# Line products of the first two tiles moved from the last slot into the second half of the slot before it, in pairs

## The chip, the cores and the metric

The kernel runs on one core of one Trainium2 chip. The core has five engines that run at the same time and wait for each other by semaphores: TensorE (matrix products; PE in the profile, its weight loads PEld), VectorE (DVE), ScalarE (ACT), GpSimd (POOL) and SyncE (SP), which here starts the DMAs. The metric is the device time of one launch in microseconds (us); lower is better.

## What is computed

The input x is [4, 1024, 128]. A local-attention feed-forward block of two layers is added to it at half weight, then a global attention layer with a memory, then the feed-forward block again. The change is in the global attention layer. Cut to what matters there:

```python
qkv = (x @ qkv_w.T + qkv_b).reshape(B, T, 3, H, dh)     # B 4, T 1024, H 16, dh 8
attn = softmax(causal(einsum('bhtd,bhsd->bhts', q, k) * scale))
seq_out = einsum('bhts,bhsd->bhtd', attn, v)
w1, w2 = x_prev @ w1w.T, x @ w2w.T                      # [B, T, H, 4]
write_lines = exterior(w1, w2)                          # 6 numbers, divided by their norm
r1, r2 = x @ r1w.T, x @ r2w.T
read_lines = exterior(r1, r2)
outer = Jw[..., :, None] * Jw[..., None, :]             # Jw from write_lines, 6 x 6 a head
M_all = decayed cumulative sum of outer over positions  # before each position
score_M = sum(einsum('bhti,bhtij->bhtj', rd, M_all) * rd)
gated = mean(sigmoid(mem_score * mem_scale) * gate)
return (seq_out + gated * mem_val) @ out_w.T + out_b
```

So the layer has two halves: an ordinary causal softmax attention, and a memory of outer products of "lines", each line being a normalised exterior product of two 4-vectors.

## The kernel before, in words

The layer is `global_attention_pass`. After the projections come two passes over the attention scores, woven together in TensorE's order. The work is cut in 16 slots (`SLOTS`): slot n is batch n // 4 and four heads. Pass 1 (`fill`, line 1712 and on) computes scores so that VectorE can take each query's maximum; pass 2 computes scores again, with the maxima folded in, for ScalarE's exponentials and the value products. A slot of pass 2 has 12 units (`U2`), each a block of 128 keys and 512, 384, 256 or 128 queries. In this text (n, u) is unit u of slot n. Widths by u: 512, 384, 256, 128, 512, 512, 512, 512, 128, 256, 384, 512.

For a unit (n, u), TensorE's order is: the scores of the next unit in two halves of two banks each (`scores`, lines 1745, 1750, 1754), each half waiting until ScalarE has read the same half of the unit before; then the value products of (n, u) (`values`, line 1769), which wait for both of ScalarE's exponentials of that unit. Between these stand pass 1's products (`produce`), which run 23 uses ahead, so that they end in unit 5 of slot 14. ScalarE does `exp` (line 2289) twice a unit, copies the finished sums (`copy_out`, line 2296) after units 0 and 4, and does the inverse roots named below.

The memory half works by tiles of 128 positions; for tile k, `w` 0 is the written line and 1 the read one. The steps are:
- `line_items` (lines 1784 and 1786, TensorE): an item is one batch of one (k, w): two f32 products of 192 columns. Tile 0 has items 0 to 7 and tile 1 items 8 to 15. Item n waits until VectorE has multiplied item n - 2. Item 0 waits for all of pass 1.
- VectorE copies one half of an item (line 2064) and multiplies it by the other (2004). After four items GpSimd's `subtract` (2231) makes the lines, VectorE squares them (2075) and sums (2010), ScalarE's `inverse(k, w)` takes the inverse root (2342, 2345), VectorE's `clip` bounds it (2014) and GpSimd's `normalise` multiplies (2243).
- GpSimd's `outer_products(k)` (2254) makes the outer products in the memory of v_all. For k = 1 it waits for all value products.
- TensorE's `tails` (1799), VectorE's `advance` (2058) and SP's `pass_state` (2491) carry the state from one tile to the next.

Every engine works its own list in order. The first two tiles' steps are written out by hand, woven into slot 15; from tile 2 on each engine runs `body(t)`, behind the slots, and TensorE's memory products (1810) and lines of tile t + 2 stand in it. The items of tiles 0 and 1 run in slot 15, one after each half of the scores, in units 0 to 7; `tails(0)` runs after unit 9, and the four inverses on ScalarE after the exponentials of units 4, 5, 9 and 10. GpSimd's list begins with a memset of the state (2259), which waits for the scores of slot 14, then `subtract(0, 0)`, `subtract(0, 1)`, `normalise(0, 0)`, `normalise(0, 1)`, `outer_products(0)`, `subtract(1, 0)`, `subtract(1, 1)`, and so on. VectorE's list is items 0 to 5, squares and sum (0, 0), items 6 and 7, squares and sum (0, 1), items 8 and 9, `clip(0, 0)`, items 10 and 11, `clip(0, 1)`, items 12 and 13, squares and sum (1, 0), items 14 and 15, squares and sum (1, 1), `advance(0)`, `clip(1, 0)`, `clip(1, 1)`.

The small arrays of these steps lie in the ring of three query/key buffers (`kq`), in parts that slots 13 and 14 have finished with.

Of the kernel before, what the change touches and what calls it, by code (L numbers as in the profile page):

```python
# [15 lines left out]
B, T = 4, 1024  # L16
# [1410 lines left out]
SLOTS = B * GROUPS  # L1427
# [5 lines left out]
S_TILES = T // TILE  # L1433
# [85 lines left out]
LINE = 6  # L1519
LROWS = AH * LINE  # L1520
ITEMS = 2 * B
# [2 lines left out]
PAIRS_6 = LINE * LINE  # L1524
HB = AH * B
HALF_READ = 9
TAILS_AT = 9
BEHIND = 3
INVERSES_AT = (4, 5, 9, 10)
CHUNK_ORDER = tuple(range(0, CHUNKS, 2)) + tuple(range(1, CHUNKS, 2))  # L1530
EARLY = CHUNKS // 2

# [17 lines left out]
def global_attention_pass(nc, C, K, A, later_keys, y, v_all, kq, probs, scratch, o_all, den_all, x):  # L1550
# [11 lines left out]
    U2 = P2_STEPS  # L1562
    QK_DMAS, M_DMAS, O_DMAS = 4 * len(JOINED), 2 * PARTS, GROUP + 1
    with ExitStack() as ctx:
# [17 lines left out]
        squares = sb("ln_s", [P, 2, CHUNK])  # L1582
# [9 lines left out]
        shared = Arena(kq[:, :, :, :].rearrange("p k w t -> p (k w t)"))  # L1592
# [1 line left out]
        shared.at = 2 * T + TILE * 2  # L1594
        left = shared.take(4 * 2 * N).rearrange("p (n c) -> p n c", n=4)
        line = shared.take(2 * HB * LINE).rearrange("p (w h b c) -> p w h b c", w=2, h=AH, b=B)
        square = shared.take(2 * HB * LINE).rearrange("p (w x c) -> p w x c", w=2, x=HB)
        ssq = shared.take(2 * HB).rearrange("p (w x) -> p w x", w=2)
        inv = shared.take(2 * HB).rearrange("p (w x) -> p w x", w=2)
        state = shared.take(2 * GROUPS * STATE_ROWS).rearrange("p (k q n) -> p k q n", k=2, q=GROUPS)  # L1600
        first = Arena(early[:, :])
# [38 lines left out]
        def item(k, w, b):  # L1640
            return ITEMS * k + B * w + b
# [32 lines left out]
        def _(pe):  # L1674
# [100 lines left out]
            def line_items(k, w, b):  # L1775
                n = item(k, w, b)
                c = b * PAD + 1 + k * TILE
                out = ps[:, LINES + n % 2, 0:4 * N].rearrange("p (f c) -> p f c", c=N)
                if n == 0:
                    pe.wait_ge(C["p1_free"], C.after("p1_free", USES))  # L1780
                if n == 2 * ITEMS:
                    wait(pe, "ml_state", 1)
                wait(pe, "ml_mul", n - 1)
                nc.tensor.matmul(out[:, 0:4:3, :], y[:, c - 1 + w:c - 1 + w + TILE], A["wlines"][:, 4 * w:4 * w + 2, :], start=True,
                                 stop=True, skip_group_check=True)
                nc.tensor.matmul(out[:, 1:3, :], y[:, c:c + TILE], A["wlines"][:, 4 * w + 2:4 * w + 4, :], start=True, stop=True,
                                 skip_group_check=True).then_inc(C["ml_proj"], 1)
# [103 lines left out]
                if 0 <= i < 2:  # L1891
                    inverse_spread(i)

            def items(n, first):
                if n == SLOTS - 1 and first < 2 * ITEMS:
                    line_items(first // ITEMS, first % ITEMS // B, first % B)

            for m in range(2):
                centre(m)
# [18 lines left out]
            for n in range(SLOTS):  # L1918
                for u in range(U2):
                    ahead = (n, u + 1) if u + 1 < U2 else (n + 1, 0)  # L1920
                    if ahead[0] < SLOTS:
                        scores(*ahead, 0)
                    for use in uses_after(n, u, 0):
                        produce(use)
                    items(n, 2 * u)
                    if ahead[0] < SLOTS:
                        scores(*ahead, 1)
                    for use in uses_after(n, u, 1):
                        produce(use)
                    items(n, 2 * u + 1)  # L1930
                    values(n, u)
                    for use in uses_after(n, u, 2):
                        produce(use)
                    if n == SLOTS - 1 and u == TAILS_AT:
                        tails(0)
# [19 lines left out]
        def _(dve):  # L1955
# [204 lines left out]
            for use in range(USES):  # L2160
                n, f = use_of(use)
# [3 lines left out]
                take_max(n, f)  # L2165
                if f == FILLS - 1:
                    neg_max(n)
            dve.wait_ge(C["p2_scores"], C.after("p2_scores", 2 * U2 * (SLOTS - 1)))
            first_items(0, 6)
            first_squares(0, 0)  # L2170
            first_items(6, 8)
# [29 lines left out]
        def _(gp):  # L2201
# [53 lines left out]
                                        w.unsqueeze(3).to_broadcast([P, HB, LINE, LINE]),  # L2255
                                        w.unsqueeze(2).to_broadcast([P, HB, LINE, LINE]), ALU.mult).then_inc(C["ml_outer"], 1)

            gp.wait_ge(C["p2_scores"], C.after("p2_scores", 2 * U2 * (SLOTS - 1)))
            nc.gpsimd.memset(state[:, :, :, :], 0.0).then_inc(C["ml_set"], 1)

            def body(t):
                if valid(t + 1):
# [4 lines left out]
                    normalise(t + 2, 0)  # L2267
                    normalise(t + 2, 1)

            for t in range(-2, S_TILES + 2):  # L2270
                body(t)
            wait(gp, "ml_m", USES_M * LAST)
            for i in range(CHUNKS):
# [6 lines left out]
        def _(act):  # L2280
# [58 lines left out]
            def inverse(k, w):  # L2339
                wait(act, "ml_ssq", 2 * k + w + 1)  # L2340
                wait(act, "ml_unit", 2 * k + w - 1)
                nc.scalar.activation(inv[:, w, :], ssq[:, w, :], ACT.Ln, bias=K["norm_bias"][:, 0:1], scale=NORM_SCALE
                                     ).then_inc(C["ml_log"], 1)
                wait(act, "ml_log", 2 * k + w + 1)
                nc.scalar.activation(inv[:, w, :], inv[:, w, :], ACT.Exp, bias=K["norm_shift"][:, 0:1], scale=-0.5
                                     ).then_inc(C["ml_inv"], 1)
# [68 lines left out]
            for n in range(SLOTS):  # L2415
                for u in range(U2):
                    exp(n, u)
                    if u == 0 and n >= 1:
                        copy_out(n - 1, 1)
                    if u == 4:  # L2420
                        copy_out(n, 0)
                    if n == SLOTS - 1 and u in INVERSES_AT:
                        inverse(*divmod(INVERSES_AT.index(u), 2))
            copy_out(SLOTS - 1, 1)
            for t in range(S_TILES - 2):
                body(t)
# [92 lines left out]
    n = CHUNKS  # L2519
# [344 lines left out]
```

## Time and profile before

| what | us |
|---|---|
| median of 3 runs | 1938.73 (1938.09 to 1938.75) |
| the profiled execution | 1937.65 |
| its span in the profile | 1935.8 |
| TensorE busy | 1876.7 (97%) |
| VectorE busy | 1609.8 (83%) |
| ScalarE busy | 1500.5 (78%) |
| GpSimd busy | 918.2 (47%) |

The profile is one execution. Its times are microseconds from the start of the span; L12 is line 12 of the kernel. The timeline gives for each engine when an instruction (or a run of like ones, xN) starts and how long it takes; starts of two instructions that follow each other without idling tell what the first one occupies, which is less than its duration, since ends overlap the next start. In square brackets stands how long the engine idled before and who ended it. The two score passes take from about 715 to 1149 us; slot 14 begins near 1092 and slot 15 near 1115.

### The profile page before, as it was taken

What the parts mean: (1) busy time and instruction counts of PE and PEld (TensorE: products, weight loads), DVE (VectorE), ACT (ScalarE), POOL (GpSimd) and SP (SyncE); (2) the same over time, 40 slices, a digit from 0 to 9 for tenths busy, and PEclk for the clock granted to TensorE, in tenths of its full rate; (3) what the DMA queues carried; (4) which work ended last, traced back from release to release, by engine and by line L of the source; (5) the groups of instructions that cost most, each with busy time, mean ns of one, the idle gap of its engine ahead of it and who ended that gap; (6) DMA issues with size and microseconds to landing.
All of it is one profiled execution on the core that took longest, in us unless ns stands there. A gap on an engine that the chain in (4) does not pass through costs nothing. (4 is left out here: it accounts for less than half of the span.)

```text
span 1935.8 us, 61266 instructions
## 1 busy us (share of the span) xinstructions
PE 1876.7 (97%) x22612; PEld 1114.6 (58%) x22612; DVE 1609.8 (83%) x5464; ACT 1500.5 (78%) x4122; POOL 918.2 (47%) x550
## 2 busy tenths in 40 slices
PE   7999999999999989999999999899999999999999
PEld 3777763577775343444444358536777635777754
DVE  6899975899995679999999859869999658999945
ACT  5999994799997353777777754459999947999973
POOL 2788860588882040000000036428888505888820
PEclk9999999999999996999999999999999999999999
DMA  6212220122121040111111000002122201221311
GB/s 186 49 44 50 46 67 6 31 48 50 45 65 26 6 154 29 42 41 42 42 42 41 25 6 2 2 10 53 45 49 49 64 6 32 47 50 44 68 23 44
DMA packets 76154, 85.63 MB, mean 44 GB/s; under 512 B 17151, under 2 KB 50515, under 8 KB 75731
## 3 DMA queue, kind: packets, MB, share of 16 engines
q1 hardware_dynamic: 75663, 81.70, 16.8%
q8 instruction: 182, 2.98, 0.6%
q14 instruction: 113, 0.93, 0.2%
q10 hardware_dynamic: 196, 0.02, 0.0%
HBM read 21.16 MB, written 8.39 MB: 15 GB/s over the span
## 5 line engine op out<-in xcount | busy, mean ns | idle before, releaser
L336 ACT ACTIVATE probs<-probs,negmax 128x128 f32<-128x128 f32 x1024 | 402.0, 402 | 1.1 <-DVE negmax L411 0.6
L2289 ACT ACTIVATE gprobs<-ps_global 128x1024 f32<-128x1024 f32 (+3 forms) x384 | 291.4, 811 | 125.0 <-PE ps_global L1754 102.4
L291 POOL TENSOR_TENSOR rot<-rot 128x1024 f32<-128x1024 f32 x128 | 302.5, 2363 | 143.2 <-DVE rot L381 143.2
L297 POOL TENSOR_TENSOR qk<-rot,cnorm 128x1024 f32<-128x1024 f32 x128 | 243.8, 1905 | 172.8 <-issue 149.0
L304 POOL TENSOR_TENSOR probs<-probs,iden 128x1024 f32<-128x1024 f32 x128 | 242.8, 1897 | 45.7 <-DVE iden L419 45.0
L1984 DVE TENSOR_REDUCE maxes<-ps_global 128x1 f32<-128x512 f32 (+2 forms) x384 | 222.0, 638 | 10.3 <-PE ps_global L1717 6.5
L411 DVE CUSTOM_DVE_ANT_0 probs<-ps_attn,masks 128x128 f32<-128x128 f32 x1024 | 226.2, 285 | 0.7 <-issue 0.5
L336 ACT ACTIVATION_READ_ACCUMULATOR probs<-probs,negmax 128x1 f32 x1024 | 204.7, 200 | 0.0
L1712 PE MATMUL ps_global<-kq 48*128 48x512 bf16 (+3 forms) x768 | 196.9, 345 | 7.2 <-DVE maxes L1984 1.8
L2219 POOL CAST m_parts<-m_turn 32x128 bf16<-32x128 f32 x16 | 4.5, 280 | 363.3 <-DVE m_turn L1998 363.3
L377 DVE TENSOR_TENSOR rot<-ps_attn,rotary 128x512 f32<-128x512 f32 x256 | 174.9, 683 | 2.1 <-PE ps_attn L202 1.6
L1769 PE MATMUL ps_global<-gprobs,v_all 128*9 128x512 f32 (+3 forms) x1536 | 160.5, 490 | 1.7 <-ACT gprobs L2289 1.7
L271 PEld LDWEIGHTS ps_attn<-probsT,v_first 128*64 128x64 f32 x2048 | 103.7, 137 | 97.7 <-ACT probsT L357 93.9
L255 PEld LDWEIGHTS ps_attn<-ident,probs 128*128 128x128 f32 x1024 | 120.3, 141 | 67.0 <-issue 64.4
L638 ACT ACTIVATE ln<-ps_attn,vecs_sb 128x512 f32<-128x512 f32 (+2 forms) x96 | 65.6, 683 | 115.9 <-PE ps_attn L600 71.7
L387 DVE TENSOR_REDUCE ssq<-sq 128x16 f32<-128x1024 f32 x128 | 154.8, 1209 | 0.3
L1980 DVE CUSTOM_DVE_ANT_0 ps_global<-ps_global,later 128x384 f32<-128x384 f32 (+1 forms) x256 | 152.2, 652 | 2.7 <-PE ps_global L1712 1.7
L1712 PEld LDWEIGHTS ps_global<-kq 48*128 48x128 bf16 x768 | 58.8, 94 | 160.2 <-DVE maxes L1984 86.4
L1745 PE MATMUL ps_global<-kq 51*128 51x512 bf16 (+3 forms) x768 | 145.3, 329 | 2.7 <-ACT gprobs L2289 1.9
L224 PE MATMUL ps_attn<-ident,qk 128*128 128x128 f32 x1024 | 141.0, 281 | 6.0 <-POOL qk L297 3.7
L282 PE MATMUL ps_attn<-oT,wo_sb 128*128 128x128 f32 x1024 | 135.2, 275 | 0.0
L255 PE MATMUL ps_attn<-ident,probs 128*128 128x128 f32 x1024 | 133.6, 274 | 0.6 <-POOL probs L304 0.6
(228 smaller groups left out, 4529.9 us busy)
## 6 DMA issues: line engine op xcount, KB each, us to landing
v_first<-v_second SPq DMA_DIRECT2D x256, 128.0 KB, 2.3
hs<-z_a SPq DMA_DIRECT2D x256, 32.0 KB, 1.9
ln<-z_b SPq DMA_DIRECT2D x56, 128.0 KB, 2.5
kq<-split_scratch SPq DMA_DIRECT2D x64, 96.0 KB
kq<-split_scratch SPq DMA_DIRECT2D x64, 64.0 KB
split_scratch<-parts SPq DMA_DIRECT2D x8, 384.0 KB, 4.1
split_scratch<-gprobs SPq DMA_DIRECT2D x6, 384.0 KB, 4.1
x_tok<-in_x_dram SPq DMA_DIRECT2D x4, 512.0 KB, 6.4
```

The lines of the kernel that those rows point to most:

```text
L255: last = nc.tensor.transpose(ps[:, b, s * TILE:(s + 1) * TILE], probs[:, k % 2, 4 * e + s, :], K["ident"][:, :])
L291: nc.gpsimd.tensor_tensor(a, a, b, ALU.add).then_inc(C["rot_sum"], 1)
L297: nc.gpsimd.tensor_tensor(qk[:, k % 2, :].rearrange("p (h d) -> p h d", d=DH), rot_a[:, k % 2, :, :], cnorm[:, k % 2, :].unsqueeze(2).to_b ...
L304: nc.gpsimd.tensor_tensor(pr, pr, iden[:, k % 2, :].unsqueeze(2).to_broadcast([P, HEADS, SPAN]), ALU.mult).then_inc(C["probs_ready"], 1)
L336: last = nc.scalar.activation(probs[:, k % 2, slot, :], probs[:, k % 2, slot, :], ACT.Exp, scale=-1.0, bias=negmax[:, k % 2, slot:slot + 1 ...
L377: nc.vector.tensor_tensor(rot_a[:, k % 2, h0:h0 + HEADS, :], x, cos, ALU.mult)
L387: nc.vector.reduce_sum(ssq[:, k % 2, :], sq[:, :].rearrange("p (h d) -> p h d", d=DH), AX_X).then_inc(C["ssq_done"], 1)
L411: nc.vector.tensor_tensor_reduce(probs[:, k % 2, slot, :], ps[:, SB0 + slot // 4, (slot % 4) * SPAN:(slot % 4 + 1) * SPAN], K["masks"][:, ...
L1712: mm = nc.tensor.matmul(out, qs[buf][rows, p, tile_cols(t)], ks[buf][rows, p, CHUNK * c:CHUNK * c + w], start=True, stop=not masked_here, ...
L1769: mm = nc.tensor.matmul(ps[32 * h:32 * h + AD + 1, O0, t0 - CHUNK * c:CHUNK], v_all[:, S_TILES * (n // GROUPS) + s, GROUP * (n % GROUPS) + ...
L1984: nc.vector.reduce_max(maxes[:, n % 2, r, p0:p1, t, c], ps[:, bank_of(use), 0:len(both) * w].rearrange("q (p s) -> q p s", s=w), AX_X).the ...
L2289: nc.scalar.activation(probs[:, step % RING, 2 * p:2 * p + 2, 0:w], ps[:, S0 + 2 * p:S0 + 2 * p + 2, 0:w], ACT.Exp).then_inc(C["p2_exp"], 1)
```

## The change

- The items start in unit 7 of slot 14 (`ITEMS_AT`), two together after both halves of the scores and ahead of the value products, up to unit 2 of slot 15.
- `tails(0)` runs after unit 6 of slot 15. The inverses run after the exponentials of (14, 10), (15, 0), (15, 2) and (15, 4).
- VectorE's wait ahead of item 0 is for the scores of slot 13, not 14.
- The squares lie in another array (`squares`, free by then), so that lines, sums and inverses all lie in the buffer that slot 13 used. The state lies in slot 14's, and GpSimd's memset of it, with its wait for the scores of slot 14, moves behind `normalise(0, 1)`.

```diff
@@ -1524,9 +1524,10 @@
-TAILS_AT = 9
+TAILS_AT = 6
+ITEMS_AT = 7
 BEHIND = 3
-INVERSES_AT = (4, 5, 9, 10)
+INVERSES_AT = ((14, 10), (15, 0), (15, 2), (15, 4))
@@ -1594,7 +1595,7 @@
         line = shared.take(2 * HB * LINE).rearrange("p (w h b c) -> p w h b c", w=2, h=AH, b=B)
-        square = shared.take(2 * HB * LINE).rearrange("p (w x c) -> p w x c", w=2, x=HB)
+        square = squares[:, :, :].rearrange("p k t -> p (k t)")[:, 0:2 * HB * LINE].rearrange("p (w x c) -> p w x c", w=2, x=HB)
@@ -1891,9 +1892,10 @@
-            def items(n, first):
-                if n == SLOTS - 1 and first < 2 * ITEMS:
-                    line_items(first // ITEMS, first % ITEMS // B, first % B)
+            def items(n, u):
+                first = 2 * (U2 * (n - SLOTS + 2) + u - ITEMS_AT)
+                for i in range(max(first, 0), min(first + 2, 2 * ITEMS)):
+                    line_items(i // ITEMS, i % ITEMS // B, i % B)
@@ -1922,12 +1924,11 @@
                     for use in uses_after(n, u, 0):
                         produce(use)
-                    items(n, 2 * u)
                     if ahead[0] < SLOTS:
                         scores(*ahead, 1)
                     for use in uses_after(n, u, 1):
                         produce(use)
-                    items(n, 2 * u + 1)
+                    items(n, u)
                     values(n, u)
@@ -2165,7 +2166,7 @@
-            dve.wait_ge(C["p2_scores"], C.after("p2_scores", 2 * U2 * (SLOTS - 1)))
+            dve.wait_ge(C["p2_scores"], C.after("p2_scores", 2 * U2 * (SLOTS - 2)))
             first_items(0, 6)
@@ -2255,8 +2256,9 @@
-            gp.wait_ge(C["p2_scores"], C.after("p2_scores", 2 * U2 * (SLOTS - 1)))
-            nc.gpsimd.memset(state[:, :, :, :], 0.0).then_inc(C["ml_set"], 1)
+            def clear_state():
+                gp.wait_ge(C["p2_scores"], C.after("p2_scores", 2 * U2 * (SLOTS - 1)))
+                nc.gpsimd.memset(state[:, :, :, :], 0.0).then_inc(C["ml_set"], 1)
@@ -2267,7 +2269,9 @@
-            for t in range(-2, S_TILES + 2):
+            body(-2)
+            clear_state()
+            for t in range(-1, S_TILES + 2):
                 body(t)
@@ -2419,8 +2423,8 @@
-                    if n == SLOTS - 1 and u in INVERSES_AT:
-                        inverse(*divmod(INVERSES_AT.index(u), 2))
+                    if (n, u) in INVERSES_AT:
+                        inverse(*divmod(INVERSES_AT.index((n, u)), 2))
```

## Rows read from the trace of the kernel before

**Rows 1.** Windows: stretch, its length, busy time of PE, PEld, DVE, ACT, POOL, PEclk, DMA share.
```profile
1106.00:1111.00 5.00, 4.11 (x64) 1.47 (x60) 0.00 (x0) 3.81 (x7) 1.11 (x3) 1.00 0.02 3
```

**Rows 2.** Timeline of PE, end of slot 14: start, length, operation, idle before.
```profile
1105.80 1.05 PE L1769 MATMUL ps_global<-gprobs,v_all 128*9 128x512 f32 x8
...
1107.75 0.23 PE L1745 MATMUL ps_global<-kq 51*128 51x128 bf16 x2 [0.60 <-ACT gprobs L2289]
...
1114.15 0.39 PE L1745 MATMUL ps_global<-kq 51*128 51x512 bf16 x2 [0.71 <-DMA kq<-m_parts]
...
1114.86 1.05 PE L1769 MATMUL ps_global<-gprobs,v_all 128*9 128x512 f32 x8
```

**Rows 3.** Timeline of PE: a lone item, then the second item of two together.
```profile
1129.19 0.59 PE L1784 MATMUL ps_global<-wlines_sb,z_a 128*128 128x192 f32 x2
1129.62 0.49 PE L1786 MATMUL ps_global<-wlines_sb,z_a 128*128 128x192 f32 x2
1130.04 1.05 PE L1769 MATMUL ps_global<-gprobs,v_all 128*9 128x512 f32 x8
...
1149.32 0.49 PE L1784 MATMUL ps_global<-wlines_sb,z_a 128*128 128x192 f32 x2
1149.64 0.49 PE L1786 MATMUL ps_global<-wlines_sb,z_a 128*128 128x192 f32 x2
1149.97 0.78 PE L1810 MATMUL ps_global<-v_all,decay 128*128 128x144 f32 x5
```

**Rows 4.** Timelines of DVE, POOL and ACT: from item 11 to the third inverse.
```profile
1133.85 0.35 DVE L2004 TENSOR_TENSOR parts<-kq,ps_global 128x192 f32<-128x192 f32 x1
...
1135.21 4.03 POOL L2254 TENSOR_TENSOR v_all<-parts 128x2304 f32<-128x2304 f32 x1
...
1140.23 0.56 DVE L2075 TENSOR_TENSOR kq<-kq 128x384 f32<-128x384 f32 x1 [2.70 <-POOL kq L2231]
1140.82 0.55 DVE L2010 TENSOR_REDUCE kq<-kq 128x64 f32<-128x384 f32 x1
...
1142.26 0.35 ACT L2342 ACTIVATE kq<-kq,norm_bias 128x64 f32<-128x64 f32 x1
```

**Rows 5.** Timeline of POOL: the memset of the state.
```profile
1112.74 1.06 POOL L2259 MEMSET kq<- 128x1152 f32 x1 [5.40 <-PE ps_global L1754]
```

**Rows 6.** Timelines of ACT and, last row, PE: exponentials, copy, inverse, value products.
```profile
1097.20 0.66 ACT L2289 ACTIVATE gprobs<-ps_global 128x256 f32<-128x256 f32 x2 [0.55 <-PE ps_global L1754]
...
1098.40 1.94 ACT L2289 ACTIVATE gprobs<-ps_global 128x1024 f32<-128x1024 f32 x2 [0.54 <-PE ps_global L1745]
1100.23 0.59 ACT L2296 COPY o_cols<-ps_global 128x512 f32<-128x512 f32 x1
...
1117.01 1.55 ACT L2289 ACTIVATE gprobs<-ps_global 128x768 f32<-128x768 f32 x2
...
1144.98 0.35 ACT L2342 ACTIVATE kq<-kq,norm_bias 128x64 f32<-128x64 f32 x1 [0.60 <-DVE kq L2010]
...
1147.59 1.04 PE L1769 MATMUL ps_global<-gprobs,v_all 128*9 128x512 f32 x8 [1.73 <-ACT gprobs L2289]
```

**Rows 7.** Timelines of DVE, SP and POOL: first item, state rows, outer products(1).
```profile
1117.21 0.36 DVE L2064 COPY kq<-ps_global 128x192 f32<-128x192 f32 x1 [11.56 <-PE ps_global L1786]
...
1144.50 2.46 SPq L2491 DMA_DIRECT2D v_all<-kq  x4
...
1148.81 4.03 POOL L2254 TENSOR_TENSOR v_all<-parts 128x2304 f32<-128x2304 f32 x1 [0.90 <-PE ps_global L1769]
```

**Rows 8.** Timeline of PE, then windows as in group 1: the granted clock.
```profile
1225.69 2.55 PE L1810 MATMUL ps_global<-v_all,decay 128*128 128x144 f32 x14 [2.19 <-DMA v_all<-kq]
...
720.00:724.00 4.00, 3.82 (x11) 0.86 (x11) 4.00 (x11) 0.00 (x0) 0.00 (x0) 0.50 0.23 70
...
1226.00:1228.00 2.00, 2.00 (x14) 2.00 (x13) 2.00 (x7) 0.91 (x4) 0.86 (x1) 0.74 0.00 0
1228.00:1230.00 2.00, 2.00 (x7) 0.98 (x6) 2.00 (x3) 1.99 (x3) 1.68 (x2) 0.50 0.01 4
```

## The prediction, made before the changed kernel was run

> **What bounds the kernel now.** A unit (n, u) is unit u of slot n. I read first the busy time by stretch [rows 1]: after pass 1 has run out in slot 14, TensorE is busy 4.11 of 5 us at the full clock and ScalarE 3.81 of 5. Then TensorE's timeline from the value products of (14, 6) to those of (14, 11) [rows 2]: it waits for ScalarE's exponentials (0.60 us ahead of the 128-wide scores) and, last, for the row of maxima from a DMA (0.71 us). So this end of slot 14 is paced by ScalarE, and it is where the change puts ten of the sixteen line items. In slot 15 the items made TensorE the bound: one unit of 512 columns there carries two items, each taking TensorE 0.85 us (1129.19 to 1130.04, [rows 3]). Behind the items, from (15, 8) on, ScalarE paces again, with two inverse roots in its queue: the one at 1144.98 waited 0.60 us for VectorE with the last exponentials behind it, and TensorE stood 1.73 us ahead of the last value products [rows 6]. So slot 15 is bound by TensorE first and ScalarE last, and what the change gains or loses stands in when its last value products end: now 1148.6.
>
> **The change, part by part.**
> The profiled execution took 1937.65 us (span 1935.8, 1.85 around it); the median is 1938.73. I work on the trace's clock and add the shift to the median.
>
> *Pairs.* A lone item costs 0.43 + 0.42 = 0.85 us of TensorE. Back to back, as the first items behind the slot run, the second takes 0.32 + 0.33 (1149.32, 1149.64, 1149.97) [rows 3]. Ahead of value products the last step is 0.42 again: a pair costs 0.43 + 0.33 + 0.32 + 0.42 = 1.50 us against 1.70. Bounds: 1.41 (as in body(0)) to 1.70; I take 1.50, made of the steps in the same surroundings.
>
> *TensorE up to item 11.* From 1105.80 to the end of the value products of (14, 11), the trace shows 36 rows, the first and last in [rows 2]; their steps free of waiting sum to 7.6 us. Five pairs add 7.5. Of the waits, that for the exponentials of (14, 7) stays (0.60 shown, 0.7 with the step it hides); the others are filled, the DMA one too. One new wait comes: inverse(0, 0) now sits behind the exponentials of (14, 10), which finish at about 1114.5, while its sum needs item 5: items 4 and 5 end at the value products of (14, 9), 1114.9, and copy, product, square and sum follow to 1116.9. So ScalarE stands 2.4 us, exponentials of (14, 11) run 1117.5 to 1119.4, and TensorE loses 0.85 us at the scores of (15, 0). Together 1105.80 + 7.6 + 7.5 + 0.7 + 0.85 = 1122.4. Scores (0.6) and the pair of (15, 0) bring its value products to 1124.5, and VectorE multiplies item 11 at 1125.1.
>
> *The chain behind item 11.* It decides. In the trace [rows 4]: product of item 11 at 1133.85, clip(0, 1), normalise(0, 1), outer products(0) 1135.21 (4.03 us on GpSimd), subtract, VectorE's square 1140.23, sum 1140.82 to 1141.37: 7.5 us. That order on GpSimd is kept, and the memset of the state, 1.06 us [rows 5], which now runs ahead of everything at 1112.74 where GpSimd is idle, is put between normalise(0, 1) and outer products(0): it joins the chain. So sum(1, 0) is ready at 1125.1 + 7.5 + 1.06 = 1133.7. Bounds of the memset's part: 0 (nothing waits) to 1.06; GpSimd runs in order and this chain has no gap, so 1.06.
>
> *Where ScalarE stands.* inverse(1, 0) was behind (15, 9), reached at 1142.26, 0.9 us after its sum [rows 4]. It is now behind (15, 2). The scores of (15, 2) go ahead of the pair of (15, 1), so ScalarE is through them at 1126.8. It waits there for 6.9 us, with exponentials (15, 3) to (15, 11) queued behind. TensorE gets on as far as the value products of (15, 2) (1130.2 to 1130.8), then needs the banks of (15, 3): ScalarE restarts at 1133.7, inverse 0.63, first half of (15, 3) 0.4: 1134.7. TensorE stands 4.0 us. Bounds of this pause: 3.4 (pairs at 1.70) to 4.3.
>
> *The rest of slot 15* is ScalarE's. From 1133.7: five 512-wide pairs at 1.83 (1098.40 to the copy at 1100.23), the 384 one 1.43 (1.55 less the 0.12 by which ends overlap), two 128 ones 0.56 (0.66 less 0.10), the 256 one 0.96 between them, one copy 0.47 (0.59 less 0.12), two inverses 1.26 [rows 6]: 14.4 us. inverse(1, 1), behind (15, 4), has its sum at 1137.2 just in time (ScalarE gets there at 1137.3). ScalarE also waits for TensorE round the narrow units, 1.8 us with the tails, now at (15, 6), ahead of them, and 0.1 early: 1150.1. The last exponential's end is 0.15 later, the value products 1.0: 1151.2. Now it is 1148.6. **Sum: +2.6 us.** The same steps laid out in the old order put the last value products at 1147.66, where the trace has 1147.59.
>
> *What lies behind.* Nothing gives this back or adds to it. outer products(1) writes where the values are read, so it starts at the last value products in either order (1148.81, 0.90 us waited for them [rows 7]) and body(0) goes on from there. The tails end near 1144.2, and SP, whose state rows are queued behind them, issues at about the time it did (1144.50 [rows 7]), now with more room before body(0). No DMA is moved past another. The new place of the squares costs nothing: the same 384 columns. VectorE's earlier start costs nothing, since it sat waiting 11.56 us there, from 1105.65 to 1117.21 [rows 7].
>
> **Rivals.**
> *Slower by over 0.2%: the pause costs the clock.* TensorE's longest pause behind pass 1 is 2.19 us, at 1225.69, and right after it the granted clock is 0.74 and then 0.50 (1.2 GHz) [rows 8]. A pause of 4.0 us is longer than any there. With TensorE's steps doubled for 4 us from 1134.7 the sum only grows by 0.35, for ScalarE is the bound and TensorE has about a fifth of each unit free. It decides if half clock lasts to 1142 or more: end 1152.6 then (+3.9), 1155.2 (+6.5) to 1147. The trace knows long stretches too (0.50 at 720 to 724 [rows 8], while TensorE was held up by VectorE). For: the pause. Against: at 1228 to 1230 TensorE was back at work and the clock came back soon. 1942.6 to 1945.2; 14%.
> The Trainium skill, "TensorE: Matmul & The Clock Gate", section "HAM oscillation — how this bites in real kernels", warns that a wait that idles TensorE long enough brings its clock down, so that the work behind the wait starts at half rate; by that rule this change would make such a wait. The trace agrees at 1225.69 [rows 8]; by the rule the sum would be +2.95 rather than +2.6.
>
> *Faster, below 0.2%: ScalarE isn't held.* If sum(1, 0) were there when ScalarE comes, the pairs and the filled waits of slot 14 would show: without inverse waits the same steps end at 1146.4, -2.2 us, 1936.5. For: no wait of this length stands in the trace, inverse(1, 0) found its sum ready. Against: outer products alone take 4.03 us of the 8.6, and ScalarE's three units to it take less than that. 8%.
>
> *Partly.* The chain overlaps more than I lay out (the first inverse not waited for, or GpSimd's steps shorter; for it speaks that GpSimd's spans are rough in a profile, against it that the same steps fit the old order): between -1 and +2; 1938 to 1940.7; 10%.
>
> *It doesn't do what it says*, i.e. items are held and start no earlier: item 0 needs all of pass 1 freed, and VectorE's last step of pass 1 ends at 1105.65 (where its 11.56 us of idling begin [rows 7]), ahead of the value products of (14, 6). Under 1%, in "partly".
>
> **How the numbers follow.** The forecast, +2.3 to +3.8 (memset, pairs at 1.70 giving +3.3, a short clock loss +0.35 on either), has 67%: 1938.73 + 2.6 = 1941.3. Measurements of this kernel differ from no change only above some 0.2%, 3.9 us. The forecast lies inside that. Slower by over 0.2%: the clock rival and the top of the forecast's range, 0.14 + 0.07 = 0.21. Faster by over 0.2% would need 3.9 us, more than the rival with no waits: 0.03. Within: 0.76. The range goes from the fast rival (1936.3) to 1943.9, which leaves out the long clock loss.
>
> **What would show it.** Right: ScalarE idle about 7 us ahead of its line 2342 between the exponentials of (15, 2) and (15, 3), ended by VectorE's sum; TensorE idle about 4 us ahead of scores, ended by ScalarE; the memset between two GpSimd steps of the chain; no idle of TensorE with items in slot 14 except about 0.7 and 0.85; items' first matmuls in pairs 0.76 us apart; last value products ending 2.6 us later; from there on the same distances. Wrong: a last value product earlier than 1148.6, an inverse that waits less than 3 us, or a stage behind slot 15 of another length by more than 1 us.

## The result

Twelve runs of the changed kernel have a median of 1940.47 us (1938.90 to 1943.75), twelve of the kernel before 1938.26 us (1934.03 to 1940.85). The medians lie 2.2 us apart; the ratio, taken over all the executions, is 1.0018, with an interval of 1.0010 to 1.0025: 3.5 us slower (1.9 to 4.9), where +2.6 was forecast. The profiled execution of the changed kernel took 1938.90 us.

The page of the changed kernel, its first two lines:

```profile
span 1937.1 us, 61266 instructions
PE 1874.7 (97%) x22612; PEld 1112.8 (57%) x22612; DVE 1609.0 (83%) x5464; ACT 1500.0 (77%) x4122; POOL 918.2 (47%) x550
```

The spans differ by 1.3 us, less than the medians, because the two profiled executions did not reach slot 14 at the same time: the value products of (14, 6) start at 1103.73 here and at 1105.80 before [rows 2]. So I compare the **stretch** from the start of those products to the end of the value products of (15, 11). Before it is 1105.80 to 1148.63, 42.8 us. After it is 1103.73 to 1149.96, 46.2 us. Behind the stretch stand 787.2 us before and 787.1 after. In this pair of executions all of the change lies in the stretch: +3.4 us.

Timeline of TensorE in the changed kernel (start, length, operation, idle before and who ended it): the start of the stretch; the pair of (15, 2) and its value products; the pause; the last value products, which answer to the last row of [rows 6].

```profile
1103.73 1.04 PE L1770 MATMUL ps_global<-gprobs,v_all 128*9 128x512 f32 x8
...
1126.52 0.59 PE L1785 MATMUL ps_global<-wlines_sb,z_a 128*128 128x192 f32 x2
1126.95 0.49 PE L1787 MATMUL ps_global<-wlines_sb,z_a 128*128 128x192 f32 x2
1127.27 0.49 PE L1785 MATMUL ps_global<-wlines_sb,z_a 128*128 128x192 f32 x2
1127.60 0.49 PE L1787 MATMUL ps_global<-wlines_sb,z_a 128*128 128x192 f32 x2
1128.01 0.62 PE L1770 MATMUL ps_global<-gprobs,v_all 128*9 128x256 f32 x8
1132.49 0.94 PE L1746 MATMUL ps_global<-kq 51*128 51x512 bf16 x4 [3.86 <-ACT gprobs L2293]
...
1148.91 1.05 PE L1770 MATMUL ps_global<-gprobs,v_all 128*9 128x512 f32 x8 [0.63 <-ACT gprobs L2293]
```

A pair goes from 1126.52 to 1128.01: it takes TensorE 1.49 us. Behind the value products TensorE stands 3.86 us, and ScalarE ends it. What held ScalarE is in its own timeline (lines 2346 and 2349 are the inverse, 2293 the exponentials):

```profile
1114.79 0.35 ACT L2346 ACTIVATE kq<-kq,norm_bias 128x64 f32<-128x64 f32 x1 [2.02 <-DVE kq L2011]
...
1123.84 1.09 ACT L2293 ACTIVATE gprobs<-ps_global 128x512 f32<-128x512 f32 x2 [0.81 <-PE ps_global L1755]
1131.44 0.35 ACT L2346 ACTIVATE kq<-kq,norm_bias 128x64 f32<-128x64 f32 x1 [6.52 <-DVE kq L2011]
1131.82 0.35 ACT L2349 ACTIVATE kq<-kq,norm_shift 128x64 f32<-128x64 f32 x1
1132.08 0.64 ACT L2293 ACTIVATE gprobs<-ps_global 128x256 f32<-128x256 f32 x2
```

The third inverse begins at 1131.44 after 6.52 us of idling, ended by VectorE's sum (line 2011), with the exponentials of (15, 3) straight behind it. In the kernel before, the inverse at 1142.26 [rows 4] had its sum already. The first inverse waited too, 2.02 us. The chain that the sum hangs on, from VectorE and GpSimd (2005 is the product of item 11, 2261 the memset, 2255 the outer products, 2011 the sum), answers to [rows 4, 5]:

```profile
1122.89 0.35 DVE L2005 TENSOR_TENSOR parts<-kq,ps_global 128x192 f32<-128x192 f32 x1
...
1124.23 1.07 POOL L2261 MEMSET kq<- 128x1152 f32 x1
1125.25 4.03 POOL L2255 TENSOR_TENSOR v_all<-parts 128x2304 f32<-128x2304 f32 x1
...
1130.85 0.55 DVE L2011 TENSOR_REDUCE kq<-ln_s 128x64 f32<-128x384 f32 x1
```

From 1122.89 to 1131.40 it takes 8.5 us, with the memset's 1.07 us in it. Last, windows, the first of the kernel before and the others of the changed one (stretch, its length, busy time of PE, PEld, DVE, ACT, POOL, granted clock, DMA share, GB/s):

```profile
1092.00:1149.00 57.00, 52.26 (x541) 22.89 (x534) 29.85 (x79) 40.26 (x61) 13.98 (x15) 1.00 0.04 7
...
1103.00:1132.00 29.00, 24.55 (x237) 14.54 (x237) 13.61 (x40) 13.73 (x23) 11.06 (x11) 1.00 0.02 5
1132.00:1139.00 7.00, 5.99 (x32) 1.00 (x36) 1.79 (x5) 6.37 (x11) 1.00 (x1) 0.55 0.05 10
1139.00:1150.00 11.00, 9.86 (x141) 3.41 (x134) 1.39 (x6) 8.18 (x12) 1.68 (x2) 0.98 0.01 3
```

In the changed kernel the granted clock falls in the middle window: for 6.8 us, from 1132.6 to 1139.5, TensorE runs at the lower of its two levels, 1.2 GHz. Before, it is 1.00 throughout both slots.

That is one execution of each. The mean granted clock over the whole program is known for all of them: 0.9837 in the twelve of the changed kernel, 0.9856 in 29 later ones of the kernel before. On 1937 us the difference of 0.0019 is 7 us at half clock (an estimate: each is on record to 0.001, and a mean of ten is uncertain by some 0.0003). So the changed kernel loses its clock as a rule, and not only in the execution that was profiled.

### The profile page after: what moved, and what is told of

Read it like the earlier page. It is cut to its first block and busy times, and to the rows that moved or that the text cites. A ratio compares the mean times of both kernels' runs of the same rounds, so it can differ in the third digit from the quotient of the medians.

```text
span 1937.1 us, 61266 instructions
## 1 busy us (share of the span) xinstructions
PE 1874.7 (97%) x22612; PEld 1112.8 (57%) x22612; DVE 1609.0 (83%) x5464; ACT 1500.0 (77%) x4122; POOL 918.2 (47%) x550
## 3 DMA queue, kind: packets, MB, share of 16 engines
q1 hardware_dynamic: 75663, 81.70, 16.9%
```

## The experiments

The theory to test: ScalarE's queue is held at the third inverse, by a chain over VectorE and GpSimd that the move of the items did not shorten. The rival: the items themselves make the slots longer, wherever the inverses stand. The second question is the clock: does the pause bring it down, and what does that cost? In all tables and texts the stretch is that of one profiled execution. Its steps repeat from kernel to kernel within hundredths of a microsecond where the order is the same and the clock full, so it can tell apart a few tenths, which the ratio of the times can't: its intervals are some 0.1% to either side, 2 us. Whether the clock falls in it can differ between executions of one kernel, so the table at the end has the mean granted clock of all of them too.

**The inverses one to three units later.**

```diff
-INVERSES_AT = ((14, 10), (15, 0), (15, 2), (15, 4))
+INVERSES_AT = ((14, 11), (15, 1), (15, 5), (15, 6))
```

> The changed kernel with the four inverse roots in ScalarE's queue behind the exponentials of (14, 11), (15, 1), (15, 5) and (15, 6); nothing else differs. Measured by the stretch from the start of the value products of (14, 6) to the end of those of (15, 11): 42.8 us before, 46.2 us in the changed kernel. Theory (ScalarE's queue is held by the third inverse, whose sum hangs on GpSimd's chain): no inverse waits, TensorE has no pause over 1 us, the clock stays at full, stretch 40.6 us, which is 2.2 us under before and 0.11% faster. Rival (the items in slot 14 themselves lengthen the slots, through TensorE's work or the score banks): stretch 45 us or more wherever the inverses stand.

Measured: stretch 41.4 us, ratio 0.9993 (0.9984 to 1.0002), against the changed kernel's 46.2 us. Four numbers in one tuple take back 4.8 us. Timelines of ScalarE (the third and fourth inverse) and TensorE (its longest idling), and the windows:

```profile
1132.12 0.38 ACT L2346 ACTIVATE kq<-kq,norm_bias 128x64 f32<-128x64 f32 x1
...
1134.84 0.35 ACT L2346 ACTIVATE kq<-kq,norm_bias 128x64 f32<-128x64 f32 x1
...
1129.09 0.39 PE L1746 MATMUL ps_global<-kq 51*128 51x512 bf16 x2 [0.63 <-ACT gprobs L2293]
...
1103.00:1129.00 26.00, 24.86 (x248) 14.53 (x244) 11.83 (x35) 14.97 (x25) 10.87 (x11) 1.00 0.03 5
1129.00:1133.00 4.00, 3.30 (x16) 0.44 (x16) 2.58 (x7) 3.84 (x7) 1.17 (x2) 0.69 0.05 8
```

No inverse waits and TensorE never stands longer than 0.63 us: the rival is out. But the stretch is 0.8 us above what was expected, and the clock falls again, for 3.4 us from about 1130, though there is no long pause. Neither theory had that. The two don't belong together, though: during the 3.4 us ScalarE waits for TensorE nowhere, and behind them only once, 0.31 us. So this fall cost 0.3 us at most, and the rest of the 0.8 us is an error in my layout. The next kernel loses its clock without a long pause too.

**Only the third and fourth inverse later.**

```diff
-INVERSES_AT = ((14, 10), (15, 0), (15, 2), (15, 4))
+INVERSES_AT = ((14, 10), (15, 0), (15, 4), (15, 5))
```

> The changed kernel with only the third and fourth inverse later, behind (15, 4) and (15, 5). Theory: the third waits 0.3 us, the fourth 1.1 us, TensorE's longest pause is 1.3 us and the clock stays at full; stretch 43.5 us, 0.7 over before, because the first inverse still holds ScalarE for 2 us behind (14, 10). Rival (only the third inverse's wait matters, the first costs nothing): stretch 42.3 us or less. Rival of the items: 45 us or more.

Measured: stretch 46.2 us, ratio 1.0013 (1.0004 to 1.0022). The longest idling of TensorE is 0.63 us, yet the clock stands at half for 10.2 us, from about 1135. Timelines of ScalarE (exponentials of (15, 3) here and with all inverses later, the fourth inverse, exponentials of (15, 8)) and TensorE (the tails), and the window:

```profile
1128.71 0.66 ACT L2293 ACTIVATE gprobs<-ps_global 128x256 f32<-128x256 f32 x2 [1.62 <-PE ps_global L1755]
...
1125.49 0.66 ACT L2293 ACTIVATE gprobs<-ps_global 128x256 f32<-128x256 f32 x2 [1.62 <-PE ps_global L1755]
...
1137.18 0.35 ACT L2346 ACTIVATE kq<-kq,norm_bias 128x64 f32<-128x64 f32 x1 [1.02 <-DVE kq L2011]
...
1144.62 0.66 ACT L2293 ACTIVATE gprobs<-ps_global 128x256 f32<-128x256 f32 x2 [3.06 <-PE ps_global L1755]
...
1141.99 2.14 PE L1800 MATMUL ps_global<-v_all,decay 128*1 128x144 f32 x32
...
1134.00:1145.00 11.00, 9.60 (x80) 2.47 (x76) 2.75 (x8) 6.89 (x11) 1.00 (x1) 0.55 0.04 9
```

The stretch is 2.7 us over the 43.5 expected, and as a whole it settles nothing on the inverses, for two things moved at once. Its first half does, for there the clock is full in all three kernels. From the start of the stretch the exponentials of (15, 3) begin after 28.35 us in the changed kernel (1132.08), 22.81 here (1128.71) and 22.08 with all inverses later (1125.49). So the third inverse's wait puts them back by 5.5 us and the first one's by 0.7. The second half shows what the clock took: at (15, 8) ScalarE waits 3.06 us for TensorE, whose tails take 2.14 us at the lower clock, where with the inverses later it waits 0.31 us there and the tails take 1.16. A pause isn't needed for the clock to fall, and the fall cost some 2.7 us here.

**The memset out of the chain.**

```diff
             def body(t):
...
                     subtract(t + 2, 1)
+                    if t == -1:
+                        clear_state()
...
-            body(-2)
-            clear_state()
-            for t in range(-1, S_TILES + 2):
+            for t in range(-2, S_TILES + 2):
                 body(t)
```

> The changed kernel with GpSimd's memset of the state moved out of the chain, behind subtract(1, 1). Theory (it lies in the chain from item 11 to the third inverse): ScalarE's wait ahead of the third inverse 1.06 us shorter, 5.5 us for 6.5, TensorE's pause 2.8 us for 3.9, stretch 45.2 us if the clock still falls for as long, 44.4 if it doesn't. Rival (the chain ends in something else, such as VectorE's order): no difference, stretch 46.2 us.

Measured: stretch 45.95 us, ratio 1.0018 (1.0009 to 1.0027). ScalarE's timeline (third inverse) and windows:

```profile
1133.75 0.35 ACT L2346 ACTIVATE kq<-kq,norm_bias 128x64 f32<-128x64 f32 x1 [5.52 <-DVE kq L2011]
...
1136.00:1143.00 7.00, 6.10 (x28) 0.79 (x28) 1.11 (x2) 6.06 (x9) 1.09 (x2) 0.55 0.06 12
```

The wait is 5.52 us, 1.00 shorter, and TensorE's pause 2.86 us, 1.00 shorter. From the start of the stretch at 1107.05 the third inverse is reached in 26.7 us, where the changed kernel takes 27.7. So the memset is in the chain with its full length. But from there to the end it takes 19.25 us for 18.52: with the same 6.8 us at half clock, 0.7 us of the gain went again, in ScalarE's waits for TensorE ahead of (15, 7) and (15, 8): 0.99 and 0.70 us, where the changed kernel has 0.34 and 0.48.

**The pause filled.**

```diff
                     for use in uses_after(n, u, 2):
                         produce(use)
+                    if n == SLOTS - 1 and u == 2:
+                        for i in range(4):
+                            nc.tensor.matmul(ps[:, M0 + 2, :], K["centre"][:, :], x[:, column(0):column(0) + CHUNK], start=True, stop=True)
```

> The changed kernel with four f32 products of 512 columns added on TensorE behind the value products of (15, 2), 3.4 us of work in the pause of 3.9 us; their results are not used. ScalarE's wait is untouched. Theory (0.8 us of the loss is the half clock that follows the pause): clock 1.00 through slot 15, stretch 45.4 us for 46.2, although TensorE has more to do. Rival (the clock costs nothing because ScalarE is the bound, and the 0.8 us is ScalarE's): stretch 46.2 us with the clock at full.

Measured: stretch 48.1 us, ratio 1.0019 (1.0007 to 1.0031). TensorE's timeline round the added products, and windows:

```profile
1132.34 3.70 PE L1937 MATMUL ps_global<-x_sb,centre 128*128 128x512 f32 x8
1136.28 0.66 PE L1746 MATMUL ps_global<-kq 51*128 51x512 bf16 x4 [0.24 <-ACT gprobs L2296]
...
1107.00:1140.00 33.00, 30.49 (x269) 16.50 (x268) 15.41 (x43) 17.64 (x31) 12.05 (x12) 1.00 0.02 4
1140.00:1147.00 7.00, 6.20 (x36) 0.95 (x36) 0.00 (x0) 5.40 (x6) 0.00 (x0) 0.54 0.06 11
```

The added products fill the pause, and TensorE stands only 0.24 us behind them. The clock stays up through the place where it fell in the changed kernel, and falls later, at about 1140.6, for 6.8 us. Neither theory said so. This execution is also the one with the lowest clock of six: their granted clocks go from 0.983, this one's, to 0.987, and their times from 1943.9 down to 1937.0 us. So with the pause filled the clock most likely falls there in some executions and not in all, and 48.1 us need not be this kernel's usual stretch. What lies there are units 4 to 7 of slot 15, from which the change took the items away and left TensorE with scores and value products only. I formed a new theory (A): the clock falls for want of TensorE's work in those units, and the items had kept it up. The next two kernels test it.

**The light units filled, with and without the pause.** One f32 product of 192 columns ahead of the value products in units 3 to 6 of slot 15:

```diff
                     items(n, u)
+                    if n == SLOTS - 1 and 3 <= u <= 6:
+                        nc.tensor.matmul(ps[:, M0 + 2, 0:192], K["centre"][:, :], x[:, column(0):column(0) + 192], start=True, stop=True)
                     values(n, u)
```

With the inverses at (14, 11), (15, 1), (15, 5), (15, 6), so without the pause:

> The kernel with the inverses behind (14, 11), (15, 1), (15, 5), (15, 6), and the same four added products of 192 columns in units 3 to 6 of slot 15. It has no long pause. Without the products the clock fell to half for 3.4 us at 1129.4 and the stretch was 41.4 us, 0.8 over what was expected. Theory A (light units): clock 1.00, stretch 41.1 us. Rival (anything else that hangs on the place of the inverses or on chance): it falls as without them, stretch 41.9 us.

In the changed kernel, so with the pause:

> The changed kernel with one f32 product of 192 columns added on TensorE ahead of the value products in each of units 3 to 6 of slot 15, where its items were taken away; the results are not used. ScalarE's wait at the third inverse, and so TensorE's pause of 3.9 us, stay. Theory A (the clock falls because units 3 to 7 of slot 15 are left with little TensorE work): clock 1.00 or a fall of at most 3.4 us; stretch 46.0 us at the full clock, the added products costing 0.5 and the kept clock giving 0.8 back. Theory B (the pause itself brings it down, as forecast): clock at half as in the changed kernel, for 6.8 us, stretch 46.8 us or more.

Windows of the first over both slots:

```profile
1107.00:1149.00 42.00, 39.30 (x413) 19.73 (x409) 16.62 (x49) 28.19 (x44) 13.75 (x14) 1.00 0.03 6
```

Without the pause the clock is 1.00 throughout (stretch 41.7 us, ratio 0.9997, 0.9988 to 1.0006), as theory A has it. But the stretch is 0.3 us longer than without the products, not shorter: the kept clock gave next to nothing back, as ScalarE's waits had shown. And over all their executions the two kernels have nearly the same mean clock, 0.9851 and 0.9853, so that the products kept the clock is shown by one execution against one. Timeline and windows of the second:

```profile
1136.18 0.67 PE L1746 MATMUL ps_global<-kq 51*128 51x512 bf16 x4 [3.87 <-ACT gprobs L2295]
...
1136.00:1142.00 6.00, 5.82 (x30) 1.52 (x32) 1.47 (x4) 5.22 (x9) 1.00 (x1) 0.58 0.05 10
1142.00:1146.00 4.00, 4.00 (x28) 1.22 (x28) 0.00 (x0) 2.59 (x3) 0.00 (x0) 0.77 0.03 6
```

With the pause of 3.87 us the clock falls right behind it, for 6.8 us, though the units are filled: theory B here. All six executions have a granted clock of 0.983 or 0.984. The stretch is 48.0 us, the ratio 1.0031 (1.0019 to 1.0042). The simplest reading of the two results is two causes, either being enough.

**Both filled.** Both additions above, in the changed kernel.

> The changed kernel with both fillings at once: four f32 products of 512 columns in TensorE's pause behind the value products of (15, 2), and one of 192 columns in each of units 3 to 6 of slot 15; their results are not used. ScalarE's wait at the third inverse stays. With the pause filled alone the clock still fell, at 1140 in the units left light; with those filled alone it still fell, right behind the pause. Theory (there are two causes, each enough by itself, and no third): clock 1.00 through slots 14 and 15, and the stretch 46.1 us, which is what the order of work costs at the full clock (45.4) and the 192-column products (0.6). Against the kernel with the light units filled alone, 48.0 us, that is the price of the fall, 1.9 us. Rival (a third cause, such as ScalarE's queue being held): it falls here too, stretch 47.5 us or more.

```profile
1133.68 0.66 PE L1746 MATMUL ps_global<-kq 51*128 51x512 bf16 x4 [0.23 <-ACT gprobs L2298]
...
1104.00:1151.00 47.00, 43.16 (x421) 21.35 (x421) 16.90 (x50) 28.19 (x45) 13.73 (x14) 1.00 0.03 5
```

The clock is 1.00 from end to end. The stretch is 46.5 us, 0.4 over the expected value, and 1.4 us shorter than with the light units filled alone, although it holds some 3.6 us more of TensorE's work (the pause of 3.87 us is 0.23 now). So the fall costs 1.4 us in this order of work. Over ten executions the mean clock is 0.9856, where the light units filled alone have 0.9835: that the pause brings the clock down is shown by more than one execution. (The ratio, 1.0021, 1.0012 to 1.0031, is no finer than the 1.4 us.)

**Pairs alone.** The kernel before, items left in slot 15.

```diff
-                    items(n, 2 * u)
                     if ahead[0] < SLOTS:
                         scores(*ahead, 1)
                     for use in uses_after(n, u, 1):
                         produce(use)
+                    items(n, 2 * u)
                     items(n, 2 * u + 1)
                     values(n, u)
```

> The kernel before, with its items left in slot 15 and its inverses where they were, but each unit's two items together behind both halves of the scores and ahead of the value products. Theory (a pair costs TensorE 1.50 us for 1.70, and adjacent scores 0.1 less): stretch 41.5 us, 1.3 under before; clock at full. Rival (being together costs nothing and gains nothing, because the second item waits for VectorE or a bank): 42.8 us.

Measured: stretch 41.6 us, 1.2 under before, the clock full:

```profile
1106.00:1148.00 42.00, 37.14 (x405) 18.56 (x405) 16.63 (x49) 28.19 (x44) 13.81 (x14) 1.00 0.03 6
```

The pairs are a good part of the change. The ratio, 1.0000 (0.9991 to 1.0009), can't show 1.2 us of 1939; the stretch can.

**Items spread.** If slot 14's end has room and slot 15's middle needs TensorE's work, the items belong in both: ten in pairs from (14, 7) on, six singly in (15, 0) to (15, 5), and inverses where their sums are there.

```diff
-INVERSES_AT = ((14, 10), (15, 0), (15, 2), (15, 4))
+INVERSES_AT = ((14, 11), (15, 1), (15, 7), (15, 8))
+ITEM_COUNTS = (2, 2, 2, 2, 2, 1, 1, 1, 1, 1, 1)
...
-                first = 2 * (U2 * (n - SLOTS + 2) + u - ITEMS_AT)
-                for i in range(max(first, 0), min(first + 2, 2 * ITEMS)):
+                k = U2 * (n - SLOTS + 2) + u - ITEMS_AT
+                counts = ITEM_COUNTS[k:k + 1] if k >= 0 else ()
+                for i in range(sum(ITEM_COUNTS[0:max(k, 0)]), sum(ITEM_COUNTS[0:max(k, 0)]) + sum(counts)):
```

> The changed kernel with items 0 to 9 in pairs in units 7 to 11 of slot 14 as there, but items 10 to 15 singly, one in each of units 0 to 5 of slot 15, and the inverses behind (14, 11), (15, 1), (15, 7) and (15, 8). Theory: no inverse waits for its sum, TensorE's and ScalarE's work are spread alike over both slots, and TensorE has an item in five of the units in which the earlier kernels of this study lost the clock (at 1129.4 with the inverses later, at 1134.2 and 1140.1 in others). Clock 1.00 throughout slots 14 and 15, stretch 38.7 us: 4.1 under before's 42.8, 0.2% faster. Rival (the clock falls wherever an inverse's or item's wait leaves TensorE short, or for a light unit at all): it falls again by 0.8 us or more, stretch 39.5 to 41.5.

Timeline of TensorE (start and last value products of the stretch), of ScalarE (third inverse) and the window over both slots:

```profile
1106.16 1.04 PE L1771 MATMUL ps_global<-gprobs,v_all 128*9 128x512 f32 x8
...
1144.26 1.05 PE L1771 MATMUL ps_global<-gprobs,v_all 128*9 128x512 f32 x8 [0.63 <-ACT gprobs L2295]
...
1137.62 0.35 ACT L2348 ACTIVATE kq<-kq,norm_bias 128x64 f32<-128x64 f32 x1
...
1106.00:1145.00 39.00, 36.89 (x404) 18.35 (x400) 16.61 (x49) 28.30 (x44) 13.76 (x14) 1.00 0.03 6
```

The stretch is 39.15 us, 3.7 under before and 7.1 under the changed kernel, 0.5 over what I expected. No inverse waits, TensorE's longest pause is 0.63 us, the clock is 1.00. The ratio is 0.9984 (0.9976 to 0.9993), 3.1 us faster than before (1.4 to 4.7): this version beats both kernels.

The table has all versions. ScalarE's waits are its idle times between instructions of the stretch, added up; the clock is the mean over all executions of the whole program, with their number.

| kernel | stretch, us | ScalarE's waits, us | TensorE's longest pause, us | at half clock in the stretch, us | mean clock (executions) |
|---|---|---|---|---|---|
| before | 42.8 | 12.8 | 1.73 | none | 0.9856 (29), 0.9857 (29), 0.9850 (13) |
| changed | 46.2 | 16.9 | 3.86 | 6.8 | 0.9837 (12) |
| inverses later | 41.4 | 12.1 | 0.63 | 3.4 | 0.9851 (11) |
| third and fourth later | 46.2 | 16.9 | 0.63 | 10.2 | 0.9841 (10) |
| memset behind | 45.95 | 16.6 | 2.86 | 6.8 | 0.9836 (10) |
| pause filled | 48.1 | 18.9 | 0.63 | 6.8 | 0.9853 (6) |
| later, light units filled | 41.7 | 12.4 | 0.63 | none | 0.9853 (10) |
| light units filled | 48.0 | 18.6 | 3.87 | 6.8 | 0.9835 (6) |
| both filled | 46.5 | 17.3 | 0.63 | none | 0.9856 (10) |
| pairs alone | 41.6 | 12.4 | 2.35 | none | 0.9848 (10) |
| items spread | 39.15 | 9.8 | 0.63 | none | 0.9849 (11) |

The three groups of the kernel before belong, in this order, to the first four kernels tried (inverses later to pause filled), to the two with the light units filled, pairs alone and items spread, and to "both filled". The three groups ran on different chips. The stretch less ScalarE's waits is 29.2 to 29.4 us in every version but before, where it is 30.0: what makes the versions differ is what ScalarE waits for.

## Why the prediction was right, and where it wasn't

- *Direction and size.* +2.6 us forecast; +3.4 in the stretch, +3.5 (1.9 to 4.9) in the times. The time lies in the range, and within 0.2%, as the likeliest of the three cases had it, though the interval reaches 0.25%.
- *The pair.* 1.50 us taken; 1.49 measured. It lies inside the bounds, 1.41 and 1.70.
- *TensorE up to item 11.* The product of item 11 was due 19.3 us into the stretch (1125.1 less 1105.80); it came at 19.2 (1122.89 less 1103.73). The sum is better than its parts: the new wait of the first inverse, 2.4 us forecast, measured 2.0, and TensorE's loss at the scores of (15, 0), 0.85 us forecast, is an idling of 0.35 us in the trace. Small errors cancelled there.
- *The chain.* 7.5 + 1.06 = 8.6 us forecast, 8.5 measured, and the kernel with the memset moved showed that its 1.06 us counts in full.
- *ScalarE's wait and TensorE's pause.* 6.9 and 4.0 us forecast, 6.5 and 3.9 measured. That the inverses' waits are the loss, and not the items, the kernel with the inverses later shows: -4.8 us. Most of it is the third one's: it puts the exponentials of (15, 3) back by 5.5 us, the first one's wait by 0.7.
- *What lies behind.* Nothing given back or added in the two profiled executions: 787.2 and 787.1 us. That they agree so closely has some luck in it, for in the profiles of the other kernels this part takes from 786.1 to 789.4 us. Outer products(1) again start at the last value products, as in [rows 7], after 4.49 us of waiting.
- *The rest of slot 15: the term that was mis-sized.* From the third inverse to the end I had 17.5 us (1151.2 less 1133.7); it was 18.5 (1131.44 to 1149.96). This step took ScalarE as the bound at the full clock. The 1.0 us parts in three. ScalarE's waits for TensorE measure 2.3 us for some 1.9 forecast; the last value products end 0.1 later; and ScalarE's own steps take 0.5 us more. Those I had each taken 0.10 to 0.12 us short for the overlap with the next one, also the six that stand ahead of a wait, where nothing overlaps: about 0.6 us by an estimate, which would be that part. The half clock's share is in the waits. While it lasts ScalarE waits 0.39 and 0.21 us, where the kernel with both places filled waits 0.27 and nothing, so 0.3 us is the clock's; the 0.34 us right behind may be too:

```profile
1133.11 1.94 ACT L2293 ACTIVATE gprobs<-ps_global 128x1024 f32<-128x1024 f32 x2 [0.39 <-PE ps_global L1746]
...
1138.17 1.94 ACT L2293 ACTIVATE gprobs<-ps_global 128x1024 f32<-128x1024 f32 x2 [0.21 <-PE ps_global L1746]
1140.45 1.94 ACT L2293 ACTIVATE gprobs<-ps_global 128x1024 f32<-128x1024 f32 x2 [0.34 <-PE ps_global L1746]
```

- *The clock rival.* Its mechanism, a pause that brings the clock down, is real: with the light units filled the clock still fell right behind the 3.87 us pause. I had a short fall as a possible +0.35 us inside the forecast, and a long one as the rival at 14%. The clock was down for 6.8 us, not the 4 us that I took from [rows 8], yet that cost 0.3 to 0.7 us, about what I had put on the short one, and the time stayed below the rival's 1942.6. The rule of the Trainium skill ("TensorE: Matmul & The Clock Gate", section "HAM oscillation — how this bites in real kernels") that a waiting TensorE loses its clock agrees with that run. But I looked at the pause only. In the trace of before, the items' products were what TensorE had to do in units 3 to 7 of slot 15, and I costed taking them away as pure relief. Three profiled kernels without a long pause lost the clock there. The wait for VectorE's sum was forecast rightly; this second way to lose the clock wasn't in the prediction at all.
- *The fast rival.* "Without inverse waits -2.2 us": measured -1.4. The clock fell for 3.4 us, but by ScalarE's waits that cost 0.3 us at most. Most of the difference is mine: the steps laid out for the later kernels were 0.5 to 0.6 us short even at the full clock (39.15 for 38.7, 41.7 for 41.1). Overlaps counted ahead of waits are the likely reason here too; that was not worked out for them.

## What to carry to other kernels

A step that is moved earlier on one engine has to be followed to every queue that holds its partner steps: here every item came forward by five units, and the third inverse by seven, from (15, 9) to (15, 2), where its sum, 8.5 us of VectorE and GpSimd behind item 11, couldn't be; there it stood in front of the exponentials that paced the slot. Place such a step where its input has already come, and take anything that isn't needed (the memset) out of its chain.

And spread the moved work rather than clear a stretch of it. The version with items in both slots was the fastest. Its clock is full in the profiled execution, but that is not the main reason: the version with the inverses later and the light units filled has the full clock and no waiting inverse too, and takes 41.7 us for 39.15. What differs is that ScalarE waits 9.8 us for 12.4, probably because TensorE's share of the work stands more evenly beside ScalarE's; the inverses' places differ too, and no kernel changes the one without the other.

## What the runs showed of the hardware

- The granted clock of TensorE fell to 1.2 GHz without any pause over 0.63 us, where slot 15's units held only scores and value products: in the profiled executions of three kernels, for 3.4, 10.2 and (with the pause filled) 6.8 us. With one f32 product of 192 columns more in each of four units, and no long pause, it stayed at 2.4 GHz in the profiles of two kernels. That the want of work is the cause is likely, not shown: the means over all executions (0.9851 without the products, 0.9853 with them; 0.9853 and 0.9856 with the pause filled) don't tell them apart. What speaks for a fall without a long pause in more than one execution is the mean of the kernel with the third and fourth inverse later, 0.9841. How much work is enough was not measured: slot 14's light end before, 4.11 of 5 us busy [rows 1], kept its clock.
- It also fell right behind a pause of 3.87 us with those units filled, in a kernel whose six executions all have a granted clock of 0.983 or 0.984; with the pause filled too the mean is 0.9856. The length of a pause alone doesn't decide: behind 2.19 us (before, at 1225.69 [rows 8]) the clock fell, behind 2.35 us (pairs alone, at 1147.2) and 2.91 us (third and fourth later, at 1235.5) it stayed at 1.00.
- A fall costs what ScalarE, which paces these units, is made to wait, and that differs. 3.4 us at half clock cost 0.3 us at most with the inverses later; 10.2 us cost some 2.7 with the third and fourth later, where they met the tails (2.14 us for 1.16); and the same 6.8 us took 0.7 us more with the memset moved than in the changed kernel.
- The profiled executions reach the value products of (14, 6) at times up to 4.1 us apart, 1103.41 to 1107.51 us, though the kernels order their work alike up to there. A difference of 3 us between two single executions says nothing here; the stretch between two marks in the trace does.
